# The value product of the last context tile, whole and in a bank of its own, in a fused attention and expert layer

## The reference, cut to what matters

```python
def _L0_xattn_ref(x, cross_input, ...):
    q, k, v = [_heads(x @ W + b) for W, b in ((Wq, bq), (Wk, bk), (Wv, bv))]
    att = jnp.einsum('bhqd,bhkd->bhqk', q, k) * scale
    att = jnp.where(causal[None, None], att, -jnp.inf)
    y = jnp.einsum('bhqk,bhkd->bhqd', jax.nn.softmax(att, axis=-1), v)
    qc, kc, vc = _heads(x @ Wcq + bcq), _heads(cross_input @ Wck + bck), _heads(cross_input @ Wcv + bcv)
    attc = jnp.einsum('bhqd,bhkd->bhqk', qc, kc) * scale
    y = y + jnp.einsum('bhqk,bhkd->bhqd', jax.nn.softmax(attc, axis=-1), vc)
    return y.transpose(0, 2, 1, 3).reshape(x.shape[0], T, C) @ Wp + bp

x = x + jnp.tanh(g_xattn[0]) * _L0_xattn_ref(_layernorm(x), ctx, ...)
x = x + jnp.tanh(g_ffn[0]) * _L0_ffn_ref(_layernorm(x), ...)
```

## Time and profile before

| | us |
|---|---|
| median of 3 runs | 1388.42 (1386.09 to 1390.41) |
| the profiled execution | 1386.87 |
| its span, first to last instruction | 1385.1 |
| PE busy | 1331.0 (96%) |
| DVE busy | 884.0 (64%) |
| ACT busy | 714.0 (52%) |
| POOL busy | 333.9 (24%) |
| L1046, exponentials, 512 of them | 494.3 |
| L1318, maximum reductions | 516.0 and 112.3 |
| L737, value products, 2432 records | 290.1 |
| L1035, copies of bank 6, 64 of them | 38.2 |
| granted clock of PE, mean | 0.994 |

### The profile page before, as it was taken

One profiled execution on the slowest core, in us unless ns is written; L12 is line 12 of the kernel. 1 busy time (PEld: TensorE's weight loads), 2 busy tenths in 40 slices (PEclk: granted clock), 3 DMA queues, 4 the chain that ended last, 5 costly groups with the idle time before them and its releaser, 6 DMA issues.

```text
span 1385.1 us, 21802 instructions
## 1 busy us (share of the span) xinstructions
PE 1331.0 (96%) x7400; PEld 661.2 (48%) x7401; DVE 884.0 (64%) x1748; ACT 714.0 (52%) x1039; POOL 333.9 (24%) x544
## 2 busy tenths in 40 slices
PE   7988999999999999999999999989999999999997
PEld 4644333333333333333333333345556777777775
DVE  6768888888888888888888888463521222222221
ACT  4645776767777777676767777732110222222221
POOL 5656111131131221211311311210000223322332
PEclk9999999999999999999999999999999999999999
DMA  7764222322322322323223223338003111221111
GB/s 242 231 200 159 73 72 74 108 94 73 119 80 83 108 73 91 106 76 105 94 69 118 83 79 107 119 99 379 0 22 119 30 30 30 33 35 31 30 30 23
DMA packets 80264, 129.09 MB, mean 93 GB/s; under 512 B 15729, under 2 KB 50289, under 8 KB 79153
## 3 DMA queue, kind: packets, MB, share of 16 engines
q1 hardware_dynamic: 71600, 117.72, 25.6%
q0 software_dynamic: 7296, 9.97, 4.6%
q10 hardware_dynamic: 1280, 0.27, 0.1%
HBM read 82.17 MB, written 45.36 MB: 92 GB/s over the span
## 4 chain that ended last, share of the span: by engine, by line
PE 87%; DMA 3%; issue 2%; ACT 1%; DVE 1%; POOL 0%; POOLq 0%; SPq 0%; ACTq 0%; DVEq 0%
PE ps L737 19%; PE ps L887 13%; PE ps L622 13%; PE ps L719 13%; PE ps L900 7%; PE ps L839 6%; PE ps L850 4%; PE ps L722 2%; PE ps L911 2%; PE ps L636 2%; DMA k_parts<-work 2%; PE ps L626 1%; PE ps L693 1%; PE ps L815 1%; PE ps L877 1%
## 5 line engine op out<-in xcount | busy, mean ns | idle before, releaser
L1046 ACT ACTIVATE arena<-ps 128x1024 f32<-128x1024 f32 (+1 forms) x512 | 494.3, 996 | 182.8 <-PE ps L719 129.9
L1318 DVE TENSOR_REDUCE mx<-ps 128x1 f32<-128x512 f32 (+1 forms) x832 | 516.0, 665 | 72.5 <-PE ps L622 59.8
L737 PE MATMUL ps<-arena 128*32 128x512 f32 (+5 forms) x2432 | 290.1, 523 | 14.7 <-issue 13.8
L1217 POOL TENSOR_SCALAR_AFFINE_SELECT arena<-arena 128x128 f32<-128x128 f32 x256 | 75.3, 294 | 573.5 <-ACT arena L1046 569.1
L622 PE MATMUL ps<-arena 96*128 96x512 bf16 x576 | 197.4, 381 | 3.4 <-DMA arena<-k_parts 2.9
L719 PE MATMUL ps<-arena 98*128 98x512 bf16 x624 | 197.7, 379 | 2.0 <-ACT arena L1046 1.6
L887 PE MATMUL ps<-arena,work 128*128 x608 | 186.4, 460 | 0.6 <-issue 0.6
L1605 DVE TENSOR_TENSOR work<-work,ps 128x352 f32<-128x352 f32 x76 | 39.6, 521 | 179.1 <-ACT work L1119 179.1
L887 PEld LDWEIGHTS ps<-arena,work 128*128 128x128 f32 x608 | 112.5, 190 | 57.4 <-issue 1.1
L1318 DVE TENSOR_REDUCE mneg<-ps 128x2 f32<-128x512 f32 (+2 forms) x192 | 112.3, 640 | 21.9 <-PE ps L632 21.9
L737 PEld LDWEIGHTS ps<-arena 128*32 128x32 f32 (+1 forms) x2432 | 58.1, 108 | 141.7 <-issue 122.9
(11 more groups left out here) (179 smaller groups left out, 1391.0 us busy)
## 6 DMA issues: line engine op xcount, KB each, us to landing
arena<-in_experts SPq DMA_DIRECT2D x8, 2176.0 KB, 15.7
o_parts<-work SPq DMA_DIRECT2D x63, 256.0 KB, 7.4
arena<-k_parts SPq DMA_DIRECT2D x48, 198.1 KB
arena<-k_parts SPq DMA_DIRECT2D x48, 132.1 KB
k_parts<-work SPq DMA_DIRECT2D x16, 300.0 KB, 4.2
q_parts<-work SPq DMA_DIRECT2D x12, 384.0 KB, 4.8
arena<-q_parts SPq DMA_DIRECT2D x48, 96.0 KB
work<-recip_rows SPq DMA_DIRECT2D x16, 256.0 KB
```

The source lines that it names most:

```text
L737: mm = pe.matmul(ps[32 * q:32 * q + VW, 6, b0:b1], vst[0:kn, r % VR, TT + kt if cross else kt, :], pr[0:kn, c0:c0 + b1 - b0], start=(phase ...
L1046: act.activation(pr[:, c0:c0 + n], ps[:, 2 * (g % 2):2 * (g % 2) + 2, :].rearrange("p b n -> p (b n)")[:, 0:n], ACT.Exp, scale=SCALE).then ...
L1217: pool.affine_select(out=exps, in_=exps, pattern=[[1, P]], compare_op=ALU.is_ge, fill=0.0, base=0, channel_multiplier=-1).then_inc(S["mask ...
L1318: return dve.tensor_reduce(m, out, AX_X, ALU.max)
```

## The change

It leaves the computed function as it is and moves sums:

- Group 5 is now X 8 and X 12, group 7 X 11, Y 2 and Y 3. Phase 2 is X 6, 7, 8 and 12, phase 3 X 9, 10, 11, Y 2 and Y 3. `MASKED` and `MASKS_BY` follow: masks 2 and 3 wait for exponential 7, phase 2 wants two masks only.
- X 12 is multiplied whole (65 rows, 512 columns), in column group 3, with `start` and `stop` both set, into the ring bank of a new entry `rest`, which stands where the second `spare` ended: in the schedule after the last maximum piece of the step, before phase 2. PE waits ahead of phase 2 for that bank's last reduction, and the maximum piece that takes the bank next waits for `rest_evac`.
- ACT copies the 32 partitions of that bank to `restsb` after exponential 7 (`rest_out`), once phase 2 is done and the head before's rows are stored (`rest_written`).
- SP stores the 17 rows of it that matter (16 numerators and the denominator, 34 KB) as a fifth piece of `o_parts`, ahead of the sums (`rest_store`). There are five denominator loads and five numerator loads for each group; h = 3 has two numerator loads instead of one.
- POOL adds one piece more, for denominators and numerators.

```diff
-          [(X, 6, 0), (X, 7, 512)], [(X, 8, 0), (Y, 2, 512), (Y, 3, 768)], [(X, 9, 0), (X, 10, 512)],
-          [(X, 11, 0), (X, 12, 512)]]
+          [(X, 6, 0), (X, 7, 512)], [(X, 8, 0), (X, 12, 512)], [(X, 9, 0), (X, 10, 512)],
+          [(X, 11, 0), (Y, 2, 512), (Y, 3, 768)]]
...
-          [(X, 6), (X, 7), (X, 8), (Y, 2)], [(X, 9), (X, 10), (X, 11), (Y, 3), (X, 12)]]
+          [(X, 6), (X, 7), (X, 8), (X, 12)], [(X, 9), (X, 10), (X, 11), (Y, 2), (Y, 3)]]
...
-MASKS_BY = [1, 2, 3, TT]
-REST_CUTS = [(0, 172), (172, 342), (342, T)]
-MASKED = [(0, 1), (1, 3), (2, 5), (3, 5)]
+MASKS_BY = [1, 2, 2, TT]
+MASKED = [(0, 1), (1, 3), (2, 7), (3, 7)]
...
         if g == 3:
-            out += [("spare", 0), ("values", 0)]
+            out += [("spare",), ("values", 0)]
         if g == 5:
-            out += [("spare", 1), ("values", 1)]
+            out.append(("values", 1))
         if g == 7:
-            out.append(("values", 2))
+            out += [("rest",), ("values", 2)]
...
+            def rest_store(v):
+
+                sp.wait_ge(S["rest_evac"], v + 1)
+                sp.dma_start(o_parts[v, P:P + D + 1, :], restsb[P - VW:P - VW + D + 1, :]).then_inc(S["rest_written"], 16)
...
                 if h == 3:
                     num_load(j, 1)
+                    num_load(j, 2)
                 if h == 4:
-                    num_load(j, 2)
-                    num_load(j, 3)
+                    num_load(j, SELF)
+                    num_load(j, REST_SUMS)
                 if h == 5:
                     recip_load(j)
+                rest_store(u)
                 sums_store(u)
...
+                if before[0] == "rest" and step >= 0:
+                    pe.wait_ge(S["rest_evac"], step + 1)
...
-                for n, (cross, kt) in enumerate(PHASES[phase]):
-                    rest = cross and kt == CT - 1
-                    kn = CTAIL if rest else P
-                    first = 0 if cross else kt * P
-                    for b0, b1, q in [(*c, q) for q, c in enumerate(REST_CUTS)] if rest else [(first, T, kt % 3 if cross else 3)]:
...
+                for cross, kt in PHASES[phase]:
+                    c0 = WHERE[cross, kt]
+                    if cross and kt == CT - 1:
+                        mm = pe.matmul(bank_of("rest")[P - VW:P, :], vst[0:CTAIL, r % VR, TT + kt, :], pr[0:CTAIL, c0:c0 + T],
+                                       start=True, stop=True, skip_group_check=True)
...
+                        if item[1] == 2:
+                            bank_free(u, "rest")
...
+            def rest_out(u):
+
+                act.wait_ge(S["pv_done"], u * NPH + 3)
...
+                    act.wait_ge(S["rest_written"], u * 16)
+                act.activation(restsb[P - VW:P, :], bank_of("rest")[P - VW:P, :], ACT.Copy).then_inc(S["rest_evac"], 1)
...
+                pool.tensor_tensor(cross_num[1], cross_num[1], cross_num[2], ALU.add).then_inc(S["num_third"], 1)
```

More of the change, by code:

```diff
@@ L88 @@
 VR = 2
+NQ = 5
+CROSS, SELF, REST_SUMS = (0, 1, 2), 3, 4
 CPAD = CT * P
@@ L111, in schedule @@
         if g == 3:
-            out += [("spare", 0), ("values", 0)]
+            out += [("spare",), ("values", 0)]
         if g == 5:
-            out += [("spare", 1), ("values", 1)]
+            out.append(("values", 1))
         if g == 7:
-            out.append(("values", 2))
+            out += [("rest",), ("values", 2)]
     return out
 PE_ORDER = schedule()
-ENTRIES = [item for item in PE_ORDER if item[0] in ("max", "spare")]
+ENTRIES = [item for item in PE_ORDER if item[0] in ("max", "spare", "rest")]
 RING = 3
@@ L247, in program @@
         DW = T // D
-        den = work[:, 0:4 * DW].rearrange("p (q t) -> p q t", q=4)
-        recip = work[:, 4 * DW:6 * DW].rearrange("p (s t) -> p s t", s=2)
+        restsb = work[:, T:2 * T]
+        den = work[:, 0:NQ * DW].rearrange("p (q t) -> p q t", q=NQ)
+        recip = work[:, NQ * DW:(NQ + 2) * DW].rearrange("p (s t) -> p s t", s=2)
         cross_recip, self_recip, self_num = [work[:, i * T:(i + 1) * T] for i in (3, 4, 5)]
-        cross_num = [shared[:, 6 * T:7 * T], shared[:, 7 * T:8 * T]]
+        cross_num = [shared[:, 6 * T:7 * T], shared[:, 7 * T:8 * T], region("wq")[:, 0:T]]
         wr_cols = sb("wr_cols", [P, 2, VW])
@@ L524, in den_load @@
                 sp.wait_ge(S["o_written"], j * (16 * GH) + 16 * h1)
+                sp.wait_ge(S["rest_written"], j * (16 * GH) + 16 * h1)
                 heads = o_parts[bass.ds(j * GH + h0, h1 - h0)]
-                for q in range(4):
+                for q in range(NQ):
                     src = heads[:, VW * q + D:VW * q + D + 1, :].rearrange("u a (d t) -> (u a) d t", t=DW)
@@ L573, in _ @@
             den_load(NGRP - 1, 0, GH - 2)
-            for q in range(4):
+            for q in range(NQ):
                 num_load(NGRP - 1, q, 0, GH - 2)
+            rest_store(NU - 2)
             sums_store(NU - 2)
             den_load(NGRP - 1, GH - 2, GH - 1)
-            for q in range(4):
+            for q in range(NQ):
                 num_load(NGRP - 1, q, GH - 2, GH - 1)
+            sp.wait_ge(S["rest_evac"], NU)
+            sp.dma_start(cross_num[2][P - D:P, :], restsb[P - VW:P - VW + D, :]).then_inc(S["num_in"], 16)
             sp.wait_ge(S["o_evac"], NU)
-            for q, dst in enumerate([yT[:, NGRP - 1, :], *cross_num, self_num]):
+            for q, dst in enumerate([yT[:, NGRP - 1, :], *cross_num[0:2], self_num]):
                 sp.dma_start(dst[P - D:P, :], osb[VW * q:VW * q + D, :]).then_inc(S["num_in"], 16)
@@ L730, in values @@
                 pe.wait_ge(S["masked"], u * TT + MASKS_BY[phase])
[L731 to L738 removed]
+                for cross, kt in PHASES[phase]:
[3 more added lines that the diff above has]
+                                       start=True, stop=True, skip_group_check=True)
+                    else:
+                        first = 0 if cross else kt * P
+                        q = kt % 3 if cross else SELF
+                        mm = pe.matmul(ps[32 * q:32 * q + VW, 6, first:T], vst[:, r % VR, TT + kt if cross else kt, :],
+                                       pr[:, c0:c0 + T - first], start=(phase == 0),
                                        stop=(phase == NPH - 1), skip_group_check=True)
@@ L1028, in _ @@
             second_part(splits[-1])
+            def rest_out(u):
+                act.wait_ge(S["pv_done"], u * NPH + 3)
+                if u == 0:
+                    for k in range(NB):
+                        act.wait_ge(scr[k], 16 * uses(k, NSPLIT))
+                else:
+                    act.wait_ge(S["rest_written"], u * 16)
+                act.activation(restsb[P - VW:P, :], bank_of("rest")[P - VW:P, :], ACT.Copy).then_inc(S["rest_evac"], 1)
             def sums_out(u):
@@ L1049, in step @@
                     if g == 1 and prev:
-                        if u == 1:
-                            for k in range(NB):
-                                act.wait_ge(scr[k], 16 * uses(k, NSPLIT))
                         sums_out(u)
@@ L1055, in step @@
                         rows(u + 1, (r + 1) % NR, rows_bank)
+                rest_out(u)
             for k in range(NB, NS):
@@ L1061, in _ @@
             act.wait_ge(S["o_evac"], NU)
-            for q in range(4):
-                src = osb[VW * q + D:VW * q + D + 1, :].rearrange("a (d t) -> a d t", t=DW)
-                act.dma_start(den[P - D:P, q, :], src).then_inc(S["den_in"], 16)
+            for q in range(NQ):
+                src, row = (restsb, P - VW + D) if q == REST_SUMS else (osb, VW * q + D)
+                act.dma_start(den[P - D:P, q, :], src[row:row + 1, :].rearrange("a (d t) -> a d t", t=DW)
+                              ).then_inc(S["den_in"], 16)
             def xn_out(b):
```

25 lines of the change are left out of this document (13 added, 12 removed).

## The result

| | before | after |
|---|---|---|
| median, us | 1388.56 (1386.09 to 1390.41, 4 runs) | 1424.37 (1423.25 to 1428.52, 4 runs) |
| ratio, 95% interval | | 1.0264 (1.0237 to 1.0292) |
| the profiled execution, us | 1386.87 | 1425.41 |
| its span, us | 1385.1 | 1423.7 |
| mean granted clock of PE | 0.994 | 0.984 |

A forecast was written before the change was run, and what follows sets the result against it. PE, busy for 96% of the span, was taken to bound the kernel. Terms of -17.9 + 5 + 0.5 + 56 + 1.5 = +45 on 1386.9 us gave 1432, stated as 1431, range 1396 to 1455.

The forecast's parts named there:

- Phase 3: PE's value phase without the six records of the thirds: 1.28 to 1.00 us, 17.9 us gained over 64 heads.
- Packing into another bank: Phase 2's whole product runs beside the others at 1.00 us; the rival that it does not: 1445 us, chance 0.05.
- The ring's wait ahead of phase 2: PE waits for DVE's reduction to free the ring bank: 0.08 us per head (0 to 0.15), 5 us in all.
- The copy: ACT's copy of the rest bank takes 0.60 us, fits ACT's 0.80 us wait for scores, free with under 0.1 to spare.
- POOL: Later masks behind three additions: nothing to 0.1 us, seven times; extra loads and addition after the last head: 0.5 us.
- The landings: New store's landing after H, SP's first stack load: 13.15 us in ordinary heads, 15.2 to 16.3 in four; copy due at 13.0.
- The rule of the turns: Each stall of ACT's copy is its excess minus the stall before: 2.2, 0.9, 2.4, 0.7, 6.2 us a group.
- the carrying over of the backlog: Busy DMA engines delay the next head's loads; full carrying raises 6.2 to 10.5 us a group; middle 8.2, 8.0 after slack.
- my own case: The store's 17 rows go to one engine and the copy waits for it: 1417 to 1450 us, chance 0.68.
- The ordinary heads: Heads outside the four stalled ones: landing 0.15 us past due, in every second one, 1.5 us in all.
- The spread store: Rival: the new store's 17 rows go to many engines, stalls of 3.75 us a group, 1399 us; chance 0.13.
- The faster case at 1374.5: Rival: the new store gets past the stack loads, landing within H + 13.0, so only the gain is left; chance 0.14.

The follow-up runs named there:

- e3: The changed kernel with the new store at 32 rows instead of 17 and two alternating buffers for the rest copy; 1373.46 us, ratio 0.9904.
- e5: The changed kernel with its 17-row store issued ahead of the group's loads, right behind its head's stack loads, one buffer; 1409.97 us, ratio 1.0162.
- e1: The changed kernel with the new store taking 32 rows (64 KB) instead of 17, nothing else different; 1392.52 us, ratio 1.0039.
- e8: The changed kernel with the new store taking 18 rows instead of 17, all else the same; 1393.71 us, ratio 1.0057.
- e6: The changed kernel with the new store at 32 rows and issued ahead of the group's loads, one buffer; 1373.21 us, ratio 0.9899.
- e2: The changed kernel with two alternating buffers for the rest copy, store still 17 rows in the same queue place; 1405.10 us, ratio 1.0125.
- e4: The changed kernel with stack loads in pieces of 16 rows, twelve per head instead of six, store of 17 rows, one buffer; 1392.60 us, ratio 1.0038.
- e9: The changed kernel with the new store taking 31 rows instead of 17, all else the same; 1465.84 us, ratio 1.0568.

## Why the prediction was right, step by step

**The direction and the mechanism held.** The forecast was +45, measured +38.5 on the profiled execution. The four stalls of a group stand where they were put: behind the stores of h = 2 to 5, ACT idle ahead of the rest copy until the store has landed, PE idle ahead of the third maximum product until the copy is done. These heads take 12.3 to 15.4 us over the stage, where 12.5 to 14.7 was forecast.

**Phase 3**: 1.28 to 1.00 forecast, 0.99 measured. **Packing into another bank**: phase 2 at 0.99 in place of 1.00, so the rival at 1445 fell. **The ring's wait ahead of phase 2**: 0.08 forecast. Phase 2 starts 0.35 after its maximum product (647.26 to 647.61), 0.31 in the kernel before, so 0.04 was paid. DVE's second reduction ends at 646.21 + 1.34 = 647.55, so the hand-over took 0.06, not the 0.10 that I took from ACT's. The sum over the stage, 5 us, was some 2.5 too much, and the undisturbed head came to 11.70 rather than 11.75.

**The copy**: 0.60 forecast for 32 partitions, 0.589 measured. It fits, as the undisturbed heads show: the trace does not bear out, for this kernel, the evacuation bound for which the prediction cited the Trainium skill, TensorEngine Tiling (Array Packing), PSUM Bottleneck.

**POOL**: nothing to 0.1 us was forecast behind the three additions, and 0.1 came (11.79 in the windows of e3). The 0.2 behind the multiplications (11.91 there) was overlooked: masks 2 and 3 move there as well, and push the three multiplications back. Together 0.3 us a group, about 2 in all.

**The landings** of the new store, from H: forecast 15.2, 16.1, 16.3, 16.1; measured 14.6, 15.85, 16.0, 15.95. The due time of 13.0 holds: the copy behind the store of h = 2 would have started at 648.76 + 11.70 = 660.46 = H + 13.0, with H at 647.45. The rule of the turns holds too, each stall being the excess minus the stall before it: 1.6, then 15.85 - 13.0 - 1.6 = 1.3, then 16.0 - 13.0 - 1.3 = 1.7, then 1.25. The rows give 1.47, 1.28, 1.61 and 1.25 (the windows above, less 11.70). So **the term that was mis-sized is the carrying over of the backlog**: I put 6.2 us without it, 10.5 with all of it, and took the middle. At full clock a group loses 5.8 to 6.7 us, POOL's 0.3 included, which is the low end: there is no sign of a further backlog on top. That lateness passes from head to head at all e5 shows (h = 6), but the landings of the earlier trace rows were read in a running kernel and would hold it already.

**What I did not foresee is the clock.** It brought the two early groups to 8.8 and 10.7 and so, by another way, some of the difference back: 53.0 us lost against undisturbed heads, where 57.5 (56 + 1.5) was forecast. Taken against the groups at full clock, the clock's share is some 7 us (an estimate: 2.5 and 4.4 in these two, under 1 in the one at 0.98). Without it the profiled execution would have been near 1418, the low end of my own case. The sum came near because two misses had opposite signs, and that is luck.

**The ordinary heads**: 0.15 in every second one was forecast. The heads that start at 638.83 and 702.94 have none (the windows above); one from 738.23 to 750.47 has 0.5. Over the whole stage they come to some 4 to 5 us beyond POOL's part, 1.5 of it in the first eight heads, which have no loads of a group; 1.5 was forecast.

**The rivals.** The spread store was put at 1399; the runs that make it so, e1 and e8, give 1392.5 and 1393.7. As a rival it was well priced, and it did not happen because 17 has no divisor up to 16 but 1. The faster case at 1374.5 asked for a store that lands within H + 13.0; e6, where it does in nearly all heads, takes 1373.2. That the sums store would be late next if only the rest copy were freed was in none of my cases, and e2 showed it: 1405 where 1373 was expected.

## What to carry to other kernels

Ahead of adding a DMA to a full queue, look at its number of rows: here one row more, even a useless one, made the kernel 31 us (18 for 17) or 73 us (32 for 31) faster. A small transfer on a busy engine also costs those that stand behind it, so a second buffer alone moves the wait to the next copy that has one buffer: clear the load or issue it earlier, and then count the waits again. With 32 rows and the store ahead of the group's loads the idea of the change pays: 1373.2 us, and 1372.6 with one of POOL's additions moved, 1% below the kernel before.

## What the runs showed that I had not expected

**Stalls that cost more than their length.** Windows around one stall of the changed kernel (columns as in the earlier trace rows, the last but two the granted clock):

```profile
250.00:256.50 6.50, 4.45 (x35) 1.53 (x27) 4.36 (x8) 2.89 (x4) 1.29 (x5) 1.00 0.37 120
256.50:259.90 3.40, 3.28 (x16) 1.25 (x16) 1.70 (x5) 2.10 (x3) 0.29 (x1) 0.50 0.46 157
```

PE's timeline there:

```profile
256.62 0.50 PE L649 MATMUL ps<-shared 96*128 96x384 bf16 x1 [2.17 <-ACT work L1057]
...
258.54 1.70 PE L754 MATMUL ps<-arena 128*32 128x512 f32 x10
260.17 0.39 PE L635 MATMUL ps<-arena 96*128 96x512 bf16 x1
```

PE had been idle for 2.17 us; then for 3.4 us its granted clock is 0.50, 1.2 in place of 2.4 GHz, and phase 3 takes 1.63 us (258.54 to 260.17) in place of 0.99. The kernel before has no such stretch between 148 and 886 us; the changed one has five, at 256.5, 283.8, 358.9, 386.2 and 591.0, each of 3.4 us but the fourth, which has 6.8. The heads in which the first four begin are 14.7 to 15.4 us long rather than 13.2. The first two of the groups shown above have two each, and lost 2 to 4 us more than those at full clock. Not every long wait brings one: PE waited 2.0 to 2.7 us ahead of L649 just before or into each of these five, and 2.0 us at 462.8 without it. In the attention stage of the other kernels there are six in e2, each behind a wait of 1.5 to 1.6 us, four in e4, thirteen in e9, one in e1 and none in e3 and e5 to e8. So part of the loss of e2, e4 and e9 is this, and not the waits alone.

**Lateness out of an almost empty DMA.** With the DMA engines busy for 0.30 to 0.34 of the time, a 34 KB store took 10.7 us to land. The share is a mean over 16 engines and can hide one that is full. The time from issue to landing of a transfer that stands behind the suspect loads is the better reading: splitting those loads alone took the median of the sums store from 8.7 to 3.4 us.
